# Householder columns of a 512-row eigenproblem: the last tile's product with x moved from VectorE to TensorE, and the filler matmuls redistributed

## The reference

```
x = _layernorm(x + _L0_gnn_ref(x, adj, ...))          # 8 Euler steps: adj @ h, h @ w_eff
deg = sum(A, 0) + sum(A, 1) - diagonal(A)
L_norm = d_inv_sqrt[:, None] * (diag(deg) - A) * d_inv_sqrt[None, :]
_, U = eigh(L_norm)
out = relu((U.T @ features) @ W1 + b1) @ W2 + b2
x = _layernorm(x + U @ out)
```

## Time and profile before

| | |
|---|---|
| time, median of 3 runs | 5413.16 us (5404.32 to 5414.88) |
| time of the profiled execution | 5403.32 us |
| its span | 5401.4 us |
| busy: PE, PEld, DVE, ACT, POOL | 51%, 39%, 79%, 18%, 17% of the span |
| granted TensorE clock, mean | 0.678 |
| Householder loop | 22 to 2961 us |
| of it, four live tiles | 22 to 944 us, k = 0 to 126 |
| three live tiles | 944 to 1830 us, k = 127 to 254 |

### The profile page before, as it was taken

How to read it: one execution, slowest core, us unless ns; L and a number is a source line. 1 busy time by engine, 2 the same in 40 slices (tenths; PEclk the granted TensorE clock), 3 DMA queues, 4 the chain that set the end, 5 groups by cost and what they waited for, 6 DMA issues and landing times.

```text
span 5401.4 us, 65645 instructions
## 1 busy us (share of the span) xinstructions
PE 2752.1 (51%) x12570; PEld 2084.9 (39%) x12571; DVE 4291.4 (79%) x24022; ACT 989.1 (18%) x4375; POOL 941.7 (17%) x4428
## 2 busy tenths in 40 slices
PE   7898888888888888886666000000000010200377
PEld 6576666655665766666665000000000000100243
DVE  7878888777777788887777888888789889899524
ACT  2322323223323333332222000000000000000000
POOL 2322222222222223333333111111000000000000
PEclk8868988787887789996555555555555555655688
DMA  1000000000000000000000000000000000000001
GB/s 43 1 1 1 1 1 1 1 1 1 1 1 1 1 1 1 1 1 1 1 1 1 26 0 0 0 0 0 0 0 0 0 0 0 0 0 0 0 0 31
DMA packets 16086, 17.23 MB, mean 3 GB/s; under 512 B 3056, under 2 KB 12400, under 8 KB 15472
## 3 DMA queue, kind: packets, MB, share of 16 engines
q1 hardware_dynamic: 15216, 13.47, 0.8%
q10 hardware_dynamic: 512, 0.02, 0.0%
HBM read 9.25 MB, written 4.19 MB: 2 GB/s over the span
## 4 chain that ended last, share of the span: by engine, by line
DVE 54%; PE 33%; issue 6%; ACT 3%; POOL 2%; DVEq 1%; ACTq 0%; DMA 0%; POOLq 0%; another core or an unknown queue 0%
DVE h L2111 5%; PE ps L736 5%; PE ps L690 3%; PE ps L786 3%; PE ps L723 3%; PE ps L668 3%; PE ps L660 3%; PE ps L646 2%; PE ps L715 2%; DVE ps L1440 2%; DVE small L1454 2%; DVE am L1353 1%; DVE hT L1738 1%; DVE h L2113 1%; DVE small L1438 1%
## 5 line engine op out<-in xcount | busy, mean ns | idle before, releaser
L690 PE MATMUL ps<-W2s,W1s 128*128 128x256 f32 x2018 | 590.7, 423 | 0.0
L736 PEld LDWEIGHTS ps<-UR 128*128 128x128 f32 x2552 | 414.7, 229 | 212.4 <-issue 105.5
L736 PE MATMUL ps<-UR 128*128 128x41 f32 (+17 forms) x2552 | 416.2, 297 | 91.1 <-ACT UR L1213 69.3
L866 PE MATMUL ps<-ident,m 128*128 128x128 f32 x36 | 9.0, 429 | 823.0 <-DVE small L2211 823.0
L810 PE MATMUL ps<-ones,qs 32*1 32x1 f32 x16 | 1.5, 158 | 821.2 <-DVE qs L1846 821.2
L690 PEld LDWEIGHTS ps<-W2s,W1s 128*128 128x128 f32 x2018 | 376.5, 205 | 41.7 <-issue 6.4
L1013 POOL TENSOR_SCALAR small<-small 128x1 f32<-128x1 f32 x511 | 117.9, 231 | 1452.7 <-ACT small L1182 1434.5
L786 PEld LDWEIGHTS ps<-small,ones 128*128 128x128 f32 x766 | 133.7, 215 | 500.7 <-DVE am L1473 497.0
L786 PE MATMUL ps<-small,ones 128*128 128x2 f32 x766 | 160.3, 279 | 324.2 <-DVE am L1473 323.6
L866 PEld LDWEIGHTS ps<-ident,m 128*128 128x128 f32 x36 | 7.0, 223 | 825.0 <-DVE small L2211 825.0
L810 PEld LDWEIGHTS ps<-ones,qs 32*1 32x1 f32 x16 | 0.7, 76 | 822.2 <-issue 822.2
(11 more groups left out here) (695 smaller groups left out, 9069.7 us busy)
## 6 DMA issues: line engine op xcount, KB each, us to landing
out<-xs SPq DMA_DIRECT2D x4, 1024.0 KB, 4.5
m<-in_adj SPq DMA_DIRECT2D x1, 1024.0 KB, 5.2
before<-c_before SPq DMA_DIRECT2D x1, 1024.0 KB, 6.1
notafter<-c_notafter SPq DMA_DIRECT2D x1, 1024.0 KB, 8.0
sib<-c_sib SPq DMA_DIRECT2D x1, 448.0 KB, 8.7
eye<-c_eye SPq DMA_DIRECT2D x1, 256.0 KB, 2.8
iota<-c_iota SPq DMA_DIRECT2D x1, 256.0 KB, 3.0
leafsel<-c_leaf SPq DMA_DIRECT2D x1, 256.0 KB, 3.2
```

The lines of the kernel that those rows point to most:

```text
L690: nc.tensor.matmul(ps[1][:, 0:2 * P].rearrange("p (a d) -> p a d", a=2), W1s[:, :], W2s[:, :].unsqueeze(1).broadcast_to([P, 2, D]), start= ...
L736: last = nc.tensor.matmul(ps[2][:, 0:2 * npend + 3], over(x_of(j)), flat[:, j, 2 * first:2 * k + 3], start=(j == tp), stop=(j == T - 1))
```

## The change

In columns with three or four live tiles TensorE forms the last tile's part of y0: `n_on` products of a 128x128 block of the matrix with the column x, added up in ps3, behind the dots and behind the one-column product L681. DVE forms one tile less. ACT copies the column from ps3 to y0 right behind the norms, and DVE waits for that copy (`y0_copied`) ahead of y. In these columns ACT's copy of an Euler group, where one is due, moves from the end of the column to just ahead of the new copy.

The streams become a table by live tiles and place: panel step 0, other panel steps with matmuls, all other columns. With four live tiles they go from 1, 1, 3 to 2, 1, 3; with three from 0, 0, 2 to 1, 1, 3; with two and with one they stay. They read `ident` in place of the weights W1s and W2s, and TensorE's wait for the weights ahead of the loop goes. The unused narrow streams go too.

```diff
-NARROW_STREAMS = (0, 0, 0, 0)
+STREAMS = {4: (2, 1, 3), 3: (1, 1, 3), 2: (0, 0, 1), 1: (0, 0, 0)}
+BY_TENSOR = 3
...
-            matmuls = bool(panel) and panel[1] < 2 + panel[4]
+            place = (0 if panel[1] == 0 else 1 if panel[1] < 2 + panel[4] else 2) if panel else 2
...
-            extra = (0, 1 if matmuls else 3, 0) if n_on == 4 else (0, 0 if matmuls else 2, 0) if n_on == 3 else                 (0, 0 if matmuls else 1, 0) if n_on == 2 else (0, 0, 0)
+            extra = (0, STREAMS[n_on][place], 0)
...
+        def product_by_tensor(k):
+
+            return window_of(k)[1] == 1 or BY_TENSOR <= window_of(k)[1]
+
+        by_tensor = [sum(product_by_tensor(c) for c in range(k + 1)) for k in range(N)]
...
-                    nc.tensor.matmul(ps[1][:, 0:2 * P].rearrange("p (a d) -> p a d", a=2), W1s[:, :],
-                                     W2s[:, :].unsqueeze(1).broadcast_to([P, 2, D]), start=True, stop=True)
+                    nc.tensor.matmul(ps[1][:, 0:2 * P].rearrange("p (a d) -> p a d", a=2), ident[:, 0:P],
+                                     ident[:, 0:P].unsqueeze(1).broadcast_to([P, 2, P]), start=True, stop=True)
...
-            pe.wait_ge(weights_loaded, 16 * 8)
...
+                if n_on > 1 and product_by_tensor(k):
+                    if k and current[k] != current[k - 1]:
+                        pe.wait_ge(panel_added, adds_done)
+                    for j in range(tp, T):
+                        last = nc.tensor.matmul(ps[3][:, 0:1], mats[current[k]][:, j, (T - 1) * P:N], x_of(j),
+                                                start=(j == tp), stop=(j == T - 1))
+                    last.then_inc(y0_ready, 1)
...
+                for _ in range(euler_units(k)[0]):
+                    next(state, None)
+                if n_on > 1 and product_by_tensor(k):
+                    act.wait_ge(y0_ready, by_tensor[k])
+                    nc.scalar.activation(y0[:, n_on - 1:n_on], ps[3][:, 0:1], ACT.Copy).then_inc(y0_copied, 1)
...
-                for _ in range(sum(euler_units(k)[0:2])):
+                for _ in range(euler_units(k)[1]):
...
-                    for i in range(n_on):
+                    for i in range(n_on - product_by_tensor(k)):
...
+                    if wide_now and product_by_tensor(k):
+                        dve.wait_ge(y0_copied, by_tensor[k])
```

More of the change, by code:

```diff
@@ L237, in eig_gnn @@
         y0_ready = sem("y0_ready")
+        y0_copied = sem("y0_copied")
         dots_ready = sem("dots_ready")
@@ L746, in _ @@
                                          start=True, stop=True).then_inc(y0_ready, 1)
-                    keep_clock_narrow(k, 0)
                     if k > narrow_from:
                         reflected_product(k - 1)
-                    keep_clock_narrow(k, 1)
                     pivot_row()
-                    keep_clock_narrow(k, 2)
                 for _ in range(euler_units(k)[1]):
@@ L794, in _ @@
                 keep_clock(halves_of[k][2])
-                keep_clock_narrow(k, 3)
             for _ in state:
@@ L1463, in householder @@
                         if not wide_now:
-                            dve.wait_ge(y0_ready, k + 1 - narrow_from)
+                            dve.wait_ge(y0_ready, by_tensor[k])
                         tt(y[:, here], source, corr[:, here], ALU.add).then_inc(y_done, 1)
```

## The result

The changed kernel takes 5330.0 us (median of 4 runs, 5315.6 to 5347.5) against 5414.0 us for the one before, a ratio of 0.985 (95% interval 0.982 to 0.988). It is faster by 84 us where 20 were forecast. Most of this document is on where the other 64 us come from, and on a part of the change that turned out to cost time.

A forecast was written before the change was run, and what follows sets the result against it. DVE was taken to bound four-tile columns, and the late root, behind TensorE's dots, three-tile ones. Terms -62 (three tiles), +38 (four tiles) and +4 (first columns) gave -20 us: 5413 to 5393 us, range 5320 to 5470.

The forecast's parts named there:

- What bounds which stage: Four tiles: columns wait for DVE. Three tiles: DVE waits for the root in 103 of 128 columns, 84.3 us.
- The clock follows the streams: Three-tile stage: added streams raise TensorE's clock to 0.97 without panel matmuls and 0.80 with them.
- the term was -62: Three-tile stage in all: -57 us in 70 columns without panel matmuls, -5 us in 58 with; bounds -190 to +77.
- 0.46 + 0.05 us for a late product and stream: Three-tile panel columns: lateness of 0.05 us at full clock plus 0.46 for the slow share of 0.40.
- the line 5.56 + 3.35 x slow share: Three-tile panel columns: 5.56 us at the full clock, plus 3.35 us for a wholly slow column.
- The product's price in slow columns: Four tiles, low clock: the new one-column product costs 1.91 us, in full where TensorE is already late.
- Sum for four tiles +38 us: Four-tile stage: -6 us in fast columns, +32 in already late ones, +12 in the rest; bounds -20 to +60.
- 4 more for the first columns: Columns 0 to 15: streams enough to make TensorE late in the first two, +4 us.
- The gain of a full-clock column: Four tiles, no panel matmuls, about 45 columns: 0.24 us at k = 24, about zero at k = 120; 0.13 taken, -6 us.
- the lateness, forecast at 32 + 12 us: Four tiles: +32 us in 17 columns where TensorE is already late, +12 us in the remaining 49 of 111.
- far more of them: Four-tile stage: expected sign that DVE waits for TensorE's sum (L791) in far more columns than now.
- 10 us as the limit: Stages behind 1830 us, untouched by the change: a move of more than some 10 us would show the prediction wrong.

The follow-up runs named there:

- streams alone: The kernel before with only the new table of streams, on the weights; DVE still forms all of y0: 5291.0 us, ratio 0.977.
- product only: The whole change with the old numbers of streams (1, 1, 3 and 0, 0, 2): 5392.2 us, 0.997 of the kernel before.
- The filler run: The kernel before with two unread one-column products wherever the new table has one stream more: 5402.1 us, ratio 0.999.
- product with four tiles only: The whole change, but with three live tiles DVE forms all of y0: 5298.8 us, 0.978 of the kernel before.
- whole change, more streams: The whole change with streams raised to 2, 2, 4; 1, 2, 4; 0, 1, 2: 5255.2 us, 0.971 of the kernel before.
- most streams: The kernel before with streams 3, 3, 3; 2, 3, 5; 1, 2, 3 and DVE forming all of y0: 5198.8 us, ratio 0.960.

## Why the prediction was right, and by how much it was off

**What bounds which stage: right.** With three tiles DVE's product less became a wait for the root. The fair comparison is with the streams alone: DVE is busy for 49 us less (642.56 to 593.85) and waits for the root 49 us more (44.1 to 93.4). Against the kernel before, the wait grew by 43 us at the old clock (product only) and by only 9 us in the whole change.

**The clock follows the streams: right. The price put on top of it: too high.** Forecast was a clock of 0.97 without and 0.80 with panel matmuls. The stage was forecast at 824 us and took 793 (786 in the second profile of the same kernel); the term was -62 and measured -93. Cut as the prediction cut it, nine and seven of each sixteen columns, and timed from root to root, the columns without panel matmuls went from 6.57 to 5.50 us (clock 0.82 to 1.00), 1.07 less where 0.82 was forecast. Those with them went from 7.37 to 7.06 us (clock 0.71 to 0.77), 0.31 less where 0.09 was forecast, although the clock rose less than assumed.

What failed in the columns with panel matmuls is the 0.46 + 0.05 us for a late product and stream, added to the line 5.56 + 3.35 x slow share. With the measured clock that line alone gives 5.56 + 3.35 x 0.46 = 7.10 us for the whole change (measured 7.06), 7.57 for product only at 0.70 (7.46) and 6.90 for streams only at 0.80 (6.77). So one line fits these kernels, with the product and without it, to 0.15 us. What the product costs with three tiles shows as a lower clock, 0.77 and 0.78 with it against 0.80 and 0.82 without it, and not on top of that. The line is a fit and doesn't say why the clock is lower.

The filler run confirms what the earlier trace rows suggested at 282:332, that filling the gap is not what does it. The Trainium skill ("TensorE: Matmul & The Clock Gate", section "Why this matters for your kernels") advises to keep TensorE continuously busy. The trace doesn't show that this is enough: with four tiles, after, TensorE is drawn busy for 789.86 of 797 us at 0.83.

**The product's price in slow columns: right where it was read, wrong in its sum.** In the long slow stretch with one-column Euler products (k = 34 to 42) the columns took 80 us before and 98 after:

```profile
272.00:352.00 80.00, 77.97 (x345) 65.61 (x345) 59.23 (x313) 19.75 (x89) 23.66 (x95) 0.59 0.00 1
352.00:944.00 592.00, 502.96 (x2531) 371.84 (x2530) 506.96 (x2873) 179.27 (x805) 126.09 (x671) 0.86 0.00 1
```

```profile
269.00:367.00 98.00, 97.46 (x419) 85.52 (x419) 55.20 (x296) 21.96 (x101) 23.86 (x96) 0.55 0.00 1
367.00:933.00 566.00, 560.33 (x3212) 441.83 (x3210) 467.01 (x2705) 194.19 (x887) 126.14 (x670) 0.88 0.00 1
```

(First before, then after.) That is 9 columns at 2.0 us, and 1.9 was the price. The stretch is as long in the other two kernels with this code, 97 and 98 us. But columns 43 to 126 went from 592 to 566 us. How much of that is chance, the same columns show in the second profile of the whole change, and then in product with four tiles only:

```profile
363.00:946.00 583.00, 580.49 (x3206) 461.46 (x3205) 466.67 (x2699) 194.77 (x886) 125.34 (x672) 0.85 0.00 1
```

```profile
370.00:953.00 583.00, 580.91 (x3213) 458.63 (x3213) 468.06 (x2706) 195.01 (x886) 125.43 (x672) 0.85 0.00 1
```

So 17 of the 26 us came in one profile only, together with its clock of 0.88. The step of the prediction that failed is "Sum for four tiles +38 us", with 4 more for the first columns: the whole stage measured -11, +2 and +9 in these three profiles. Two of its terms were mis-sized. The gain of a full-clock column was taken as 0.13 us and was about 0.5 at k = 24, because the timeline's drawn lengths were added where the start-to-start times hold (1.38 for the streams and 0.89 for the product, not 1.54 and 0.96). Over the 54 columns without panel matmuls from 43 on, the column went from 6.55 to between 6.09 and 6.29 us; the two kernels with the same streams and no product there have 6.32 and 6.43. And the lateness, forecast at 32 + 12 us, was smaller: DVE's wait for TensorE's sum went from 16.9 to 43.2 us, and to 51.5 and 53.8 in the other two, 26 to 37 us more. It stood in 30, 37 and 39 columns instead of 28, not in far more of them, as I had named for a sign.

Two small slips in the working had no weight: at k = 120 its own numbers give a loss of 0.16 us and not zero, and 0.72 + 0.43 - 1.13 is 0.02 and not 0.05. Each moves the sum by some 4 us.

**The fixed stages.** The two-tile stage grew by 13 us with its code unchanged; I had named 10 us as the limit. Across the kernels with the old or new numbers of streams and no other change there, it took 628 to 643 us with clocks of 0.89 to 0.92. So its length follows the clock, and how the clock comes out there depends on something that isn't in that stage's code. What can be said is where: 12 of the 13 us lie in the 32 columns with panel matmuls, which have no streams (5.27 to 5.64 us, clock 0.86 to 0.77); the other 96 took 461 and 463 us. What moves the clock there stays open. The same holds for the differences of up to 20 us between four-tile stages that differ in no product and no number of streams.

**The net.** By the ratios the streams of the change are worth 110 to 127 us, and the product takes 47 to 64 back and returns 7 to 18, if anything. My forecast had the sign of both. It gave the streams too little, and it gave the product too high a price in slow columns. Both errors have the same sign, so nothing cancelled: the range held the result because it was 150 us wide, not because the sum was good.

## What to carry to other kernels

When a serial loop leaves TensorE idle and its clock goes up and down, price filler matmuls by the clock of the stretches that have them, not by the gap that they fit in: here the best of the kernels tried overfills the gap of the three-tile columns. Look first at the columns that have few or no streams; most of the last gain lay there. Fill with wide streams; one-column products of about the same length left the whole time as it was. Before moving work to an engine with room, look at which wait ends last in each stage and at the engine's low clock, since the room disappears there first; and add start-to-start times, not drawn lengths. A single profile of a stage is no measure of 10 or 20 us: two profiles of one kernel differed by 13 us there.

## What the runs showed of the hardware

In stretches of mostly one-column float32 products TensorE was drawn busy for 99 to 100% of the time, at a granted clock of 0.51 (282:332, before) and 0.55 (269:367, after). Filler of that kind left the three-tile stage at 0.79, where wide streams of about the same length brought 0.90. Streams on a mostly zero operand did as well as on the weights: 5297 and 5291 us, a clock of 0.90 in both.

At the full clock the sum starts 1.38 us after the first of three streams of 256 float32 columns, 1.80 to 1.81 after the first of four and 2.24 after the first of five, where TensorE is what it waits for. Rows of the whole change (k = 24), of whole change, more streams, and of most streams:

```profile
210.42 1.54 PE L698 MATMUL ps<-ident 128*128 128x256 f32 x6
211.80 0.34 PE L791 MATMUL ps<-small,ones 128*128 128x2 f32 x2
...
1000.12 1.97 PE L698 MATMUL ps<-ident 128*128 128x256 f32 x8
1001.92 0.28 PE L791 MATMUL ps<-small,ones 128*128 128x2 f32 x2
...
1054.50 2.40 PE L691 MATMUL ps<-W2s,W1s 128*128 128x256 f32 x10
1056.74 0.30 PE L787 MATMUL ps<-small,ones 128*128 128x2 f32 x2
```

So each further stream takes 0.43 us of TensorE's time, as the prediction had it. The four one-column products of k = 24 take 0.89 us from their first start to that of the next group, 0.22 each.
